# Two attention layers on one core: a rewoven prologue, side work moved to other places of the second attention, and a tail in halves

## The reference, cut to what matters

```python
xn = layernorm(x)
s = xn + attention0(layernorm(xn) * gamma + beta)      # no mask
y = square(relu(xn @ W_fc.T)) @ W_proj.T               # 512 hidden
g = silu(spikes(y) / 5)                                # five steps of a leaky spiking unit
x = x + s * g
xn = layernorm(x)
s = attention1(xn)                                     # causal, with a position slope for each head
g = silu(coupling(xn))                                 # three cycles of a small gelu network that turns xn
out = x + s * g
```

## Time and profile before

| | |
|---|---|
| median of 3 runs | 959.24 us (958.57 to 959.48) |
| the profiled execution | 960.38 us, span 958.6 us |
| ScalarE busy | 836.5 us, 87% |
| TensorE busy | 811.0 us, 85% |
| VectorE busy | 412.2 us, 43% |
| GpSimd busy | 178.3 us, 19% |

### The profile page before, as it was taken

The page is one execution under the profiler, slowest core; times in us unless marked ns, Lnnn a source line. Parts: engine busy times, 40 slices in busy tenths (PEclk is TensorE's granted clock), DMA queues, the critical chain, the costliest instruction groups (busy, mean ns, idle before and its releaser), DMA issues. The chain is left out here.

```text
span 958.6 us, 23599 instructions
## 1 busy us (share of the span) xinstructions
PE 811.0 (85%) x10046; PEld 329.2 (34%) x10046; DVE 412.2 (43%) x874; ACT 836.5 (87%) x951; POOL 178.3 (19%) x218
## 2 busy tenths in 40 slices
PE   2847999899999999999999988837778788888876
PEld 1412333333343433433334342213233333333332
DVE  7632244635457554574455776771112111121222
ACT  5736999999999999999999955638999999999995
POOL 1101110103112031111311111001223232233132
PEclk9777999999999999999999999978999999999998
DMA  6773020020200302003001042010202102012000
GB/s 173 242 242 86 2 69 5 1 72 2 71 25 23 116 1 72 29 19 116 2 1 40 30 139 84 0 45 1 71 1 83 57 27 82 27 57 83 13 1 23
DMA packets 32050, 53.55 MB, mean 56 GB/s; under 512 B 5576, under 2 KB 16456, under 8 KB 31944
## 3 DMA queue, kind: packets, MB, share of 16 engines
q1 hardware_dynamic: 31944, 52.02, 17.2%
HBM read 31.29 MB, written 20.71 MB: 54 GB/s over the span
## 5 line engine op out<-in xcount | busy, mean ns | idle before, releaser
L938 ACT ACTIVATE a_probs<-a_sc 128x1024 f32<-128x1024 f32 x512 | 474.5, 1032 | 19.1 <-PE a_sc L1129 18.6
L1805 ACT ACTIVATE a_probs<-a_sc 128x1024 f32<-128x1024 f32 (+1 forms) x320 | 274.7, 958 | 35.0 <-PE a_sc L1932 20.3
L1144 PE MATMUL a_o<-a_probs,vt 128*18 128x256 f32 (+1 forms) x3072 | 271.4, 456 | 0.0
L1129 PE MATMUL a_sc<-q_st,k_st 32*128 32x512 f32 x1024 | 131.4, 501 | 26.2 <-ACT a_probs L938 17.6
L1967 PE MATMUL a_o<-a_probs,vt 128*18 128x256 f32 (+3 forms) x1920 | 153.3, 429 | 0.0
L1926 PE MATMUL a_sc<-q_st,k_st 32*128 32x512 f32 (+3 forms) x768 | 80.7, 427 | 66.6 <-ACT a_probs L1805 54.6
L1144 PEld LDWEIGHTS a_o<-a_probs,vt 128*18 128x18 f32 x3072 | 65.3, 97 | 143.4 <-issue 103.5
L1129 PEld LDWEIGHTS a_sc<-q_st,k_st 32*128 32x128 f32 x1024 | 50.6, 183 | 140.6 <-ACT a_probs L938 127.9
L1831 POOL TENSOR_SCALAR_AFFINE_SELECT a_probs<-a_probs 128x512 f32<-128x512 f32 x96 | 59.7, 643 | 208.4 <-ACT a_probs L1805 208.4
L1926 PEld LDWEIGHTS a_sc<-q_st,k_st 32*128 32x128 f32 x768 | 38.0, 184 | 131.4 <-ACT a_probs L1805 115.6
L1853 DVE STREAM_TRANSPOSE a_turn<-a_o 128x512 f32<-128x512 f32 x16 | 11.5, 717 | 151.2 <-PE a_o L1967 151.2
(11 more groups left out here) (231 smaller groups left out, 754.7 us busy)
## 6 DMA issues: line engine op xcount, KB each, us to landing
q_st<-q_hl SPq DMA_DIRECT2D x48, 256.0 KB
k_st<-k_hl SPq DMA_DIRECT2D x48, 256.0 KB
q_hl<-parts SPq DMA_DIRECT2D x12, 512.0 KB, 4.4
k_hl<-parts SPq DMA_DIRECT2D x12, 512.0 KB, 4.8
q_hl<-p_parts SPq DMA_DIRECT2D x4, 512.0 KB, 4.1
k_hl<-p_parts SPq DMA_DIRECT2D x4, 512.0 KB, 5.1
out_dram<-x SPq DMA_DIRECT2D x7, 256.0 KB, 4.5
x<-in_L_attn_x_dram SPq DMA_DIRECT2D x3, 512.0 KB, 6.0
```

The costliest lines, as they stand in the source:

```text
L938: nc.scalar.activation(probs[t % RING][:, 2 * pair:2 * pair + 2, :], scores[unit % SLOTS][:, :, :], ACT.Exp).then_inc(expd, 1)
L1129: ins = nc.tensor.matmul(scores[(2 * t + i // 2) % SLOTS][:, i % 2, :], k_st[part, g, kt * P:(kt + 1) * P], q_st[part, g, qh * HALF:(qh + ...
L1144: ins = nc.tensor.matmul(o_ps[32 * h:32 * h + 2 * W9, c0:c1], vt[b % 2][:, kt, gp, h, W9 * gs:W9 * gs + 2 * W9], probs[t % RING][:, h, c0: ...
L1805: nc.scalar.activation(probs[t % RING][:, 2 * pair:2 * pair + 2, 0:width(t)], scores[unit % SLOTS][:, :, 0:width(t)], ACT.Exp).then_inc(ex ...
```

## The change

**Prologue.** The moments are taken in three groups (tiles 0 to 7, 8 to 19, 20 to 31), and statistics of later tiles, low parts and the bias of V stand between root steps. ScalarE zeroes only the nine columns between the two V parts, in front of its first copy, and GpSimd writes the ones without waiting. TensorE transposes half m+1 behind the products of half m, so that the products of half 1 do not stand behind the transposes of half 2. GpSimd normalizes halves 6 and 7. SP's closing waits are gone, and the second part of batch 0's Q and K is loaded in `first_attention`. Four buffers now live through the program (`early`, `ext`), and the attention and `middle` use them in place of their own; where they are used first, VectorE waits for the stores that read them.

**First attention.** V of batch 1 is formed in pairs 23 and 24 of batch 0, no longer 1 and 2; the weights are scaled in pairs 9 and 13, no longer 0 and 4; GpSimd does the first squares ahead of its first wait for the weights.

**Second attention.** Other pairs for `z`, `mix`, the gates and the tanh; GpSimd's `update(b, 0)` comes behind the last mask of the batch; in the last batch GpSimd multiplies the bias by the gate and adds it to x ahead of time. The tail works in halves of 256 columns: projections of the first group of heads are done by TensorE while VectorE settles, into four PSUM banks of the scores.

```diff
@@ first_attention's and prologue's shared buffers
+                "early": [sb0(f"early{n}", [P, 2, 2, HALF], F32R) for n in range(2)],
+                "ext": [sb0(f"ext{side}", [P, T]) for side in range(2)],
@@ prologue, SP
-                    if m in (2, 3):
-                        if m == 2:
-                            sp.wait_ge(s["ext_kept"], 32)
...
-                        load_pair(sp, s, 0, 0, m - 2, s["staged"][0][m - 2])
-                    if m == 4:
+                        load_pair(sp, s, 0, 0, 0, s["staged"][0][0])
+                    if m == 3:
                         sp.wait_ge(ext_rdy, 1)
...
-                for hf in range(2):
-                    sp.wait_ge(stored[hf], 64)
-                sp.wait_ge(s["ext_kept"], 64)
@@ prologue, GpSimd
-                pool.wait_ge(v_zero, 1)
...
+                pool.wait_ge(rooted, 1)
+                for m in range(6, M):
+                    for t in range(HT):
+                        n = HT * m + t
+                        ins = pool.tensor_scalar(hs[:, n, :], s["x"][:, n, :], s["mean"][:, n:n + 1], rstd[:, 0, n:n + 1],
+                                                 ALU.subtract, ALU.mult)
+                    ins.then_inc(hs_late, 1)
@@ prologue, ScalarE
+                for n in range(2):
+                    between = s["vt"][n][:, :, :, :, W9:2 * W9].rearrange("p t g j w -> p (t g j) w")
+                    ins = nc.scalar.activation(between, idle[:, :, 0:W9].broadcast_to([P, BT * 2 * G, W9]), ACT.Copy, scale=0.0)
+                ins.then_inc(v_zero, 1)
                 h_kept(0)
...
                     for z in range(2):
+                        if m >= 2 and z == 1 and m + 1 < M:
+                            h_kept(m + 1)
...
-                    if m + 2 < M:
-                        h_kept(m + 2)
                     if m == 1:
-                        for n in range(2):
-                            flat = s["vt"][n][:, :, :, :, :].rearrange("p t g j w -> p (t g j w)")
...
+                        h_kept(2)
@@ prologue, VectorE
-                token_moments(BT, NT)
+                ch.after(spread_of(2 * BT, FIRST))
+                moments_of(BT, FIRST)
+                for k in range(ROOT_STEPS):
+                    root(BT, FIRST, k)
+                    spread_of(FIRST + k, FIRST + k + 1)
+                    ch.wait()
                 normalized(2)
+                low_of(0, 0)
+                low_of(0, 1)
+                low_of(1, 0)
+                low_of(1, 1)
                 normalized(3)
+                normalized(4)
+                ch.after(spread_of(FIRST + ROOT_STEPS, NT))
+                moments_of(FIRST, NT)
+                for k in range(ROOT_STEPS):
+                    root(FIRST, NT, k)
+                    if k == 2:
...
+                    if k in (5, 8):
+                        low_of(2, k // 8)
+                    ch.wait()
+                ratios()
+                normalized(5)
@@ prologue, TensorE
-                    if m + 2 < M:
-                        turn(m + 2)
+                    if m >= 1 and m + 1 < M:
+                        turn(m + 1)
@@ side_fills
-        if b + 1 < B:
+        if 0 < b < B - 1:
             fill("v0", b + 1, 0, 1)
             fill("v0", b + 1, 1, 2)
...
+        if b == 0:
+            fill("v0", 1, 0, 23)
+            fill("v0", 1, 1, 24)
@@ first_attention
                 keep_last(sp, s, [s["stored02"], s["stored03"]])
+                load_pair(sp, s, 0, 0, 1, staged[1])
...
-                    if b == 0 and r == 0:
+                    if b == 0 and r == 9:
                         dve.wait_ge(s["wo_in"], 16 * 10)
...
-                    if b == 0 and r == 4:
+                    if b == 0 and r == 13:
@@ second_fills
-            fill("z", b, 0, 5)
-            fill("z", b, 1, 6)
-            fill("mix", b, 0, 16, 17)
-        else:
-            fill("tail", b - 1, 0, 1)
-            fill("tail", b - 1, 1, 2)
+            fill("z", b, 0, 7)
+            fill("z", b, 1, 8)
+            fill("mix", b, 0, 17, 18)
@@ second_attention
-    TANH_AT = (16, 18)
-    GATE_AT = (10, 11)
+    TANH_AT = (19, 25)
+    GATE_AT = (11, 14)
...
-                    if r == 36:
+                    if b == B - 1 and r == 30:
+                        pool.wait_ge(gated, 2 * B)
+                        pool.tensor_tensor(mix[1][:, :, :], s["y"][:, tiles(b, 1), :], s["bo"][:, 1:2, :].broadcast_to([P, HT, C]),
+                                           ALU.mult).then_inc(lifted, 1)
+                        pool.wait_ge(lifted, 1)
+                        x = s["x"][:, tiles(b, 1), :]
+                        pool.tensor_tensor(x, x, mix[1][:, :, :], ALU.add).then_inc(lifted, 1)
+                    if r == PER1 - 1:
                         update(b, 0)
+
+                pool.wait_ge(gained, 1)
+                x = s["x"][:, tail_tiles(0), :]
+                pool.tensor_tensor(x, x, mix[1][:, 0:2, :], ALU.add).then_inc(tailed[0], 1)
...
+                def settle_last(k):
+                    cols = slice(HALF // 2 * k, HALF // 2 * k + HALF // 2)
...
+                    ends.after(nc.vector.transpose(t, o_ps[:, cols]))
+                    ends.after(nc.vector.reciprocal(inverse, used[:, :, :, D]))
+                    ends.after(nc.vector.tensor_tensor(
+                        used, used, inverse.rearrange("p n (s o) -> p n s o", o=1).broadcast_to([P, HALF // 64, 2, W9]), ALU.mult))
+                    nc.vector.transpose(on[ENDS - 1][:, cols], t).then_inc(tail_on, 1)
+
+                def gain(k):
...
+                    nc.vector.tensor_tensor(mix[1][:, 2 * k:2 * k + 2, :], banks, s["y"][:, tail_tiles(k), :], ALU.mult).then_inc(gained, 1)
...
+                dve.wait_ge(pv_done, S)
+                settle_last(0)
+                settle_last(1)
+                gain(0)
+                gain(1)
+                dve.wait_ge(gained, 2)
+                x = s["x"][:, tail_tiles(1), :]
+                nc.vector.tensor_tensor(x, x, mix[1][:, 2:4, :], ALU.add).then_inc(tailed[1], 1)
@@ second_attention, TensorE
+                for t in range(HT):
+                    nc.tensor.matmul(tail_banks[t], on[1][:, t * P:(t + 1) * P], s["wo_x1"][:, 0, :], start=True, stop=False)
+                for k in range(2):
+                    pe.wait_ge(tail_on, k + 1)
+                    for t in (2 * k, 2 * k + 1):
+                        ins = nc.tensor.matmul(tail_banks[t], on[ENDS - 1][:, t * P:(t + 1) * P], s["wo_x1"][:, 1, :], start=False, stop=True)
+                    ins.then_inc(tail_ps, 1)
```

211 lines of the change are left out of this document (113 added, 98 removed).

## The result

The changed kernel takes 936.98 us (median of 4 runs, 935.77 to 938.43), the kernel before 959.36 us beside it (4 runs, 958.57 to 960.07). The ratio is 0.9768 with a 95% interval of 0.975 to 0.9785: 22.4 us, 2.3%, faster. The forecast was 934.0 with a range of 926 to 944. The changed kernel was timed once more with the second set of experiments: 937.75 us (5 runs, 936.99 to 938.56), ratio 0.9768 (0.9749 to 0.9786).

The account below looks back on a forecast made before the run. ScalarE's exponentials set the pace, so gains were sought where it runs none. Gains of 12.1+7.9+3.8+1.5 = 25.3 us gave 935.1 from the profiled execution and 933.9 from the median, stated as 934.0; range 926 to 944.

Parts of the forecast that it names:

- Term 1: Prologue and hand-over: the attention's first VectorE work comes at 56.3 against 68.36 us, 12.1 gained (7 to 14.5).
- half 4 at 33.4: Prologue: ScalarE starts half 4 at 33.4 us, after half 3 at 29.7, in rounds of 3.5 to 4.1.
- The 2.1 that I added for contention: Prologue: GpSimd beside VectorE delays the flag, 1.3 us for eight normalizations and 0.8 for two casts, to 53.5.
- rival (e): Prologue: SP still ends it, held by full queues, and VectorE's later wait returns the rest; within 0.2% of before; chance 0.02.
- Term 2: First attention's start: the gap at 80 to 89.6 goes, one near 0.9 us may stay; 7.9 gained (5.5 to 8.8).
- rival (c): First attention's start keeps half its loss: TensorE at low clock, extra loads crowding queues; 4 us more, 938; chance 0.07.
- Term 3: Second attention: new placement saves 1.17 us per batch, 0.9 lost at mask 31; 3.8 gained (1.5 to 5).
- Term 4: Tail: last addition 2.35 us sooner, less 0.85 for a half product meeting GpSimd's update; 1.5 gained (0.8 to 2.5).
- Rival (a): Prologue stays longer: two low-clock TensorE stretches, or ScalarE waiting for stores behind the load; 5 us more, 939; chance 0.15.
- (b): GpSimd holds VectorE for all its new work; 2.5 us more, 936.5; chance 0.10.
- (d): Second attention: the placement only moves the gaps, its gain falls to -0.9, giving 938.7; chance 0.06.
- (f): Slower: TensorE's clock stays low far into the first attention; with fifteen pairs (95 us) the time is 973; chance 0.03.

Follow-up runs that it names:

- peak_before_root: Changed kernel with VectorE's first maximum taken before the third root instead of after half 5 is normalized: 933.79 us, ratio 0.9722 to the kernel before.
- old_places: Changed kernel with the second attention's side work back in its old places, halved tail kept: 941.88 us, ratio 0.9798 to the kernel before.
- all_on_vector: Changed kernel with halves 6 and 7 normalized by VectorE instead of GpSimd: 936.54 us, ratio 0.9753 to the kernel before.
- weights_waited_early: Changed kernel with batch 1's V pieces in pairs 1 and 2 and VectorE waiting for output weights at steps 0 and 4: 947.10 us, ratio 0.9873.
- v_pieces_early: Changed kernel with batch 1's V pieces back in pairs 1 and 2, weights still scaled late: 934.86 us, ratio 0.9726 to the kernel before.
- filler_only: Changed kernel plus the early V pieces' TensorE products in pairs 1 and 2, results unread, real pieces staying in pairs 23 and 24: 934.76 us, ratio 0.9736.
- all_mended: Changed kernel with first maximum before the root, V pieces in pairs 1 and 2, and GpSimd's last-batch rise and update earlier: 932.29 us, ratio 0.9702.

## Why the prediction came out as it did

The forecast of 934.0 was 3.0 under the result, which lies in its own range (929 to 939) and in the whole one. Of the 25.3 us of the sum, 21.9 came in the profiled execution, which is 1.5 us over the median of its kernel. The order of the four terms and their mechanisms held. No rival as a whole took place; two steps were mis-sized.

- **Term 1, 12.1 forecast, 10.7 measured.** The step that failed is "half 4 at 33.4". I let ScalarE's rounds follow each other from half 3 on and did not ask what TensorE needs for its sums of squares: the tile that VectorE's maximum frees, and VectorE's program has that maximum behind the third root and half 5. Half 4 came at 37.36, 4.0 late, 1.6 of it from its products at the low clock (3.62 us for 1.98), though I had taken the low level for half 2 only. peak_before_root moved that one reduction: the products took 1.96 and half 4 came at 34.09. The round I took as 3.5 to 4.1 was 3.56 at the end (half 6 at 45.50, half 7 at 49.07), which gave part back: half 7 was 3.6 late. The 2.1 that I added for contention was nearly all wrong as a cost at the flag: the casts took some 1.3 of VectorE (0.61+1.01 less twice 0.17), but the root's eleven steps, 17.15 to 20.33, took 0.29 each with their bn_stats and not 0.39, so the third half was in time; and the eight tiles on GpSimd held VectorE by 0.1. 51.4+3.6 = 55.0 against a flag at 54.8: the wait that I had left out and the contention that did not come offset each other in part, so that the flag's miss of 1.3 (54.8 for 53.5) is smaller than either error. That is luck. The price of a tile on GpSimd was off too, 6.29/8 = 0.79 and not 0.32, with no effect since the tiles were wanted later.
- **The hand-over and SP: right.** 2.83 after the flag, no closing wait. The four stores and the load of the second part were 13 issues, not 16, and ended 10.4 us after the memset for 10. That SP would be next, rival (e), is false for this kernel and true 3 us further on.
- **Term 2, 7.9 forecast, 5.0 measured, the largest miss.** Some 1.9 of these 2.9 us are the execution's: from the memset to the 13th exponential old_places and all_on_vector took 14.4 and 14.3 us with the same program, which would be a gain of 6.9. The step that failed in all five profiles is "one gap under 1 us", with TensorE at the low clock: the first gap is 1.5 to 1.6 in each. The move of both side pieces was taken as pure relief. In truth the 6.11 us gap went because the scaling moved behind the load's end (weights_waited_early: 12.2 us if it does not), and the move of the pieces took work from TensorE that it needed there: 2.5 to 3.0 us in the times (v_pieces_early, filler_only), with the clock back at 64.6 and 66.5 for 67.6 to 73.8 without it. With the pieces early one gap of 0.66 is what is left, just what the forecast said of the other placement. It is the first half of rival (c) at its mechanism, 1.0 to 2.9 of the 4 it was priced at; the part about the extra loads is not borne out, since filler_only runs the same loads.
- **Term 3, 3.8 forecast, 4.3 measured.** 74.66 to 73.42 is 1.24 per batch for 1.17, and the loss at mask 31 is 0.78 for 0.9 (a gap of 0.91, of which 0.13 stays when GpSimd's operations are moved). 4 x 1.24 less 0.78 is 4.2. old_places, which gives the tail 0.6 back, lost 4.5 in its time.
- **Term 4, 1.5 forecast, 1.8 measured.** The half product was held by GpSimd for 0.64, not 0.85, since GpSimd's operation had begun 0.48 earlier; the last addition ended 5.4 behind the last product for 5.7.
- **Rival (a)** came in part: a second stretch at the low clock (32.8 to 39.6) made half 4's products 1.6 longer, of the 5 us it was priced at; no engine waited for stores. **(b)** fell for the tiles and held for the casts; **(d)** and **(f)** fell: the low clock lasted 9 to 15 us into the attention, not 63.

Left open: at which moment the clock falls and rises at the start of the attention. The same program had it low for 13.6 us there in two profiles and for 20.5 in three, and one profile of each kernel can't say how often each comes. That more work for TensorE there helps is shown (filler_only), but not why the clock fell at 48.9 in all_mended and at 54.3 in v_pieces_early to rise at 66.0 and at 64.6, nor how much work would be enough; a filler of the right size, placed from the hand-over to the first products without delaying a score, was not tried.

## What to carry to other kernels

When a chain gets faster, walk through the PSUM tile that each producer reuses and find, in program order, the instruction that frees it: a 0.7 us reduction behind a long block of other work cost 2 to 3 us here. When the pace is set by another engine but TensorE has just been idle, do not take its side work away from the first microseconds: products, even useless ones, put in behind the first scores gained 3 us, while twice as many in front of them, 6.0 us of work, lost 4. A late place for an instruction that waits for a load can be worth most of the wait (12 of 19 us here), so when loads are added in front, check that place first. And before a microsecond in one stage of a profile is put down to an edit, look at the same stage in profiles whose edits lie elsewhere: here it moved by up to 1.9 us by itself.

## What the runs showed of the hardware that was not expected

- A VectorE tensor_scalar of 128x12 took 0.61 and 1.01 us under a GpSimd cast of 48x1024 (1.02 us each), 0.17 alone; four tensor_scalars of 128x128 took 1.21 us beside a GpSimd tensor_scalar of the same size and 1.11 alone. The first kind has constants as scalars, the second a scalar for each partition.
- GpSimd needs 0.79 us for a tensor_scalar of 128x128 float32; VectorE 0.28.
- The attention's first VectorE work follows 2.83 us after the last engine's work where VectorE was last, and 3.5 us after SP's last DMA issue where SP was (52.0 to 55.49).
- With the same program in the attention, the granted clock was back at 1.00 from 72.7 to 73.8 us in three profiled executions and from 67.6 and 68.7 in two, and the 13th exponential came 14.8 and 13.0 us after the first. With 32 records more for TensorE at 62.8 and 32 at 68.2 us the clock was back from 66.5, in v_pieces_early from 64.6.
